# Split weights kept in an HBM scratch tensor, the mix's tanh ahead of the exponentials, and half of the hidden low parts on GpSimd

## The reference

```python
x = x + attn_a(layernorm(x))      # linear attention with a recurrence, 32 heads of 4
x = x + ffn(layernorm(x))         # 8 experts, summed
x = x + attn_b(layernorm(x))      # softmax attention, 16 query heads, one key head
x = x + ffn(layernorm(x))         # the same 8 experts again

def expert_step(acc, w):          # ffn; wg, wu: 128 x 512, wd: 512 x 128
    wg, wu, wd = w
    h = silu(x @ wg) * (x @ wu)
    return acc + h @ wd, None

mix = softmax((x @ Wmix.T + bmix).reshape(b, t, NH, 2), axis=-1)   # in attn_a
```

## Time and profile before

| | us |
|---|---|
| median of 3 runs | 1833.79 (1830.01 to 1835.16) |
| the profiled execution | 1834.89 |
| its span, first to last instruction | 1833.1 |
| mean granted clock of TensorE | 0.962 |
| DMA, mean over the span | 59 GB/s, 108.96 MB in all |

### The profile page before, as it was taken

The page is one execution under the profiler, slowest core; times in us unless marked ns, Lnnn a source line. Parts: engine busy times, 40 slices in busy tenths (PEclk is TensorE's granted clock), DMA queues, the critical chain, the costliest instruction groups (busy, mean ns, idle before and its releaser), DMA issues. The chain is left out here.

```text
span 1833.1 us, 25467 instructions
## 1 busy us (share of the span) xinstructions
PE 1653.8 (90%) x7232; PEld 1256.6 (69%) x7232; DVE 1188.0 (65%) x1999; ACT 1195.3 (65%) x2231; POOL 1235.1 (67%) x1025
## 2 busy tenths in 40 slices
PE   3597989888998989998699999996999999999998
PEld 2365766667676767786366666664788888888887
DVE  5668788786959677564466666662555555555554
ACT  2245565756575655776287787785677777777776
POOL 3576676767776667767177777776566666666665
PEclk8799999999999999999699999998999999999999
DMA  3011222212122222332000000000233333333331
GB/s 116 1 52 53 69 58 64 69 52 70 58 64 66 67 58 69 105 93 63 1 1 1 1 2 0 1 1 18 71 100 96 102 94 100 103 92 103 94 98 52
DMA packets 115177, 108.96 MB, mean 59 GB/s; under 512 B 7003, under 2 KB 81888, under 8 KB 115040
## 3 DMA queue, kind: packets, MB, share of 16 engines
q1 hardware_dynamic: 115040, 107.39, 19.8%
HBM read 105.27 MB, written 2.10 MB: 59 GB/s over the span
## 5 line engine op out<-in xcount | busy, mean ns | idle before, releaser
L465 POOL TENSOR_TENSOR ARENA_R<-ARENA,ARENA_R 128x512 fp32r<-128x512 f32 x384 | 558.7, 1457 | 347.3 <-ACT ARENA_R L460 345.5
L557 DVE TENSOR_TENSOR ARENA<-ARENA,pair 128x512 f32<-128x512 f32 x512 | 349.2, 682 | 407.6 <-PE pair L340 341.0
L517 ACT ACTIVATE ARENA<-bank 128x512 f32<-128x512 f32 x512 | 304.9, 595 | 305.8 <-PE bank L340 305.0
L338 PE MATMUL pair<-ARENA_R 128*128 128x512 f32 x1064 | 423.8, 398 | 54.0 <-ACT ARENA L919 24.4
L340 PE MATMUL pair<-ARENA_R 128*128 128x512 f32 x1064 | 417.0, 392 | 0.0
L339 PE MATMUL pair<-ARENA_R 128*128 128x512 f32 x1064 | 417.0, 392 | 0.0
L527 ACT ACTIVATE ARENA_R<-ARENA 128x512 fp32r<-128x512 f32 x512 | 319.5, 624 | 89.4 <-DVE ARENA L557 88.5
L533 DVE TENSOR_TENSOR ARENA_R<-ARENA,ARENA_R 128x512 fp32r<-128x512 f32 x384 | 314.7, 820 | 0.0
L842 POOL TENSOR_TENSOR ARENA_R<-ARENA,ARENA_R 128x512 fp32r<-128x512 f32 x192 | 249.4, 1312 | 80.3 <-ACT ARENA L1027 76.8
L338 PEld LDWEIGHTS pair<-ARENA_R 128*128 128x128 f32 x1064 | 201.9, 190 | 118.7 <-ACT ARENA L919 27.7
L338 PE MATMUL bank<-ARENA_R 128*128 128x512 f32 x568 | 241.1, 424 | 21.6 <-DVE ARENA L1503 15.6
(11 more groups left out here) (213 smaller groups left out, 2201.1 us busy)
## 6 DMA issues: line engine op xcount, KB each, us to landing
ARENA<-in_L_ffn_Wg_dram SPq DMA_DIRECT2D x128, 256.0 KB, 2.6
ARENA<-in_L_ffn_Wu_dram SPq DMA_DIRECT2D x128, 256.0 KB, 2.6
ARENA<-in_L_ffn_Wd_dram SPq DMA_DIRECT2D x128, 256.0 KB, 2.7
X<-in_L_attn_a_x_dram SPq DMA_DIRECT2D x8, 256.0 KB, 5.4
out_dram<-X SPq DMA_DIRECT2D x8, 256.0 KB, 3.4
CST<-in_tables_dram SPq DMA_DIRECT2D x1, 835.5 KB, 4.6
ARENA<-in_tables_dram SPq DMA_DIRECT2D x1, 768.0 KB, 4.6
CST<-in_tables_dram SPq DMA_DIRECT2D x1, 256.0 KB, 4.7
```

The costliest lines, as they stand in the source:

```text
L338: pe.matmul(dst, wh, xh, start=start, stop=False)
L465: g.tensor_tensor(WL[:, x % 2, part, :], WS[:, x % 2, part, :], WH[:, x % 2, part, :].bitcast(F32), ALU.subtract).then_inc(F.wl, 1)
L517: act.activation(SG[:, c % 2, :], bank[c % 2], ACT.Silu).then_inc(F.sil, 1)
L557: v.tensor_tensor(HF[:, c % FC, :], SG[:, c % 2, :], bank[2 + c % 2], ALU.mult).then_inc(F.mul, 1)
```

## The change

A scratch tensor `split_weights` in HBM holds for each of the eight experts and three parts the high and the low part side by side (512 KB a part). WH and WL become one buffer W2 of the same total size, two experts deep. Only for x < 8, the first feed-forward tile, are weights split on the chip; SyncE then stores each part (`store_split`). After all stores have landed, SyncE loads the split parts of expert x % 8 straight into W2 (`load_split`), each when TensorE has finished that part of expert x - 2. TensorE waits for the load instead of for GpSimd (`weights_ready`). The splitting at the end of attention b goes; the first load of block two waits there for the last `stack2` (q2_ready), as the splitting did.

`hidden_lo` is made by VectorE for even steps and by GpSimd for odd ones. The mix's tanh moves from step 10 to step 8, ahead of the exponentials. The projection v3 moves from step 11 to step 12.

```diff
--- before.py
+++ after.py
@@ -275,8 +275,7 @@
 
         XTH = take(2, TOK, dt=F32R)
         XTL = take(2, TOK, dt=F32R)
-        WH = take(2, 3, FFN, dt=F32R)
-        WL = take(2, 3, FFN, dt=F32R)
+        W2 = take(2, 3, 2, FFN, dt=F32R)
         HH = take(FC, TOK, dt=F32R)
         HL = take(FC, TOK, dt=F32R)
         LAH = take(12, P, dt=F32R)
@@ -313,7 +312,7 @@
         b_used = {n: sem(f"b_{n}_used") for n in BPROJ}
         B = sems("b", "u_q u_k hi lo v_ready v_used st_ready st_used kst_ready kst_used row_ready row_used nmh nml "
                       "q2_ready q2_used t_ready t_used pl vhi pv os turn oc ro o ot otc out done")
-        F = sems("f", "wload0 wload1 wh wl gate up sil mul hh hl hlp d ys back done")
+        F = sems("f", "wload0 wload1 store0 store1 sg su sd wh wl gate up sil mul hh hl hlp d ys back done")
         stored = sem("stored")
         carried = sem("carried")
 
@@ -322,6 +321,7 @@
 
             eng.sem_inc(carried, 1)
 
+        split = nc.dram_tensor("split_weights", [NE, 3, P, 2, FFN], F32, kind="Internal").ap()
         x_tok = a_x.rearrange("b t c -> (b t) c").rearrange("(n s p) c -> p n s c", n=NT, p=P)
         o_tok = out.rearrange("b t c -> (b t) c").rearrange("(n s p) c -> p n s c", n=NT, p=P)
 
@@ -439,7 +439,7 @@
 
         def lo_done(G):
 
-            return (F.hlp, G // FC + 1) if G % FC == FC - 1 else (F.hl, (FC - 1) * (G // FC) + G % FC + 1)
+            return (F.hlp if G % 2 else F.hl, G // 2 + 1)
 
         def base(G):
             return 0 if G < NT * CH else NT * CH
@@ -457,19 +457,39 @@
 
             act.wait_ge((F.wload0, F.wload1)[x % 2], 48 * (x // 2 + 1))
             after(act, (F.gate, F.up, F.d)[part], FC * (x - 1))
-            act.activation(WH[:, x % 2, part, :], WS[:, x % 2, part, :], ACT.Copy).then_inc(F.wh, 1)
+            after(act, (F.store0, F.store1)[x % 2], 48 * (x // 2))
+            act.activation(W2[:, x % 2, part, 0, :], WS[:, x % 2, part, :], ACT.Copy).then_inc(F.wh, 1)
 
         def lo_part(g, x, part):
 
             g.wait_ge(F.wh, 3 * x + part + 1)
-            g.tensor_tensor(WL[:, x % 2, part, :], WS[:, x % 2, part, :], WH[:, x % 2, part, :].bitcast(F32),
-                            ALU.subtract).then_inc(F.wl, 1)
+            g.tensor_tensor(W2[:, x % 2, part, 1, :], WS[:, x % 2, part, :],
+                            W2[:, x % 2, part, 0, :].bitcast(F32), ALU.subtract).then_inc(F.wl, 1)
+
+        def store_split(sp, x, part):
+
+            sp.wait_ge(F.wl, 3 * x + part + 1)
+            sp.dma_start(split[x, part], W2[:, x % 2, part, :, :].bitcast(F32)).then_inc((F.store0, F.store1)[x % 2], 16)
+
+        def load_split(sp, x, part):
+
+            landed = (F.sg, F.su, F.sd)[part]
+            after(sp, landed, 16 * (x - NE))
+            sp.wait_ge((F.gate, F.up, F.d)[part], FC * (x - 1))
+            sp.dma_start(W2[:, x % 2, part, :, :].bitcast(F32), split[x % NE, part]).then_inc(landed, 16)
+
+        def weights_ready(pe, x, part):
+
+            if x < NE:
+                pe.wait_ge(F.wl, 3 * x + part + 1)
+            else:
+                pe.wait_ge((F.sg, F.su, F.sd)[part], 16 * (x - NE + 1))
 
         def part_at(f, c):
 
             x = NE * f + c // FC + 1
             part = c % FC - 1
-            return None if part < 0 or x == NE * NT or x == 2 * NE * NT else (x, part)
+            return None if part < 0 or x >= NE else (x, part)
 
         def ffn_pe(pe, f, c):
 
@@ -478,14 +498,14 @@
             if c == 0:
                 pe.wait_ge(n_f.lo, f + 1)
             if k == 0:
-                pe.wait_ge(F.wl, 3 * x + 1)
+                weights_ready(pe, x, 0)
             after(pe, F.sil, G - 1)
-            split_product(pe, bank[c % 2], WH[:, u, 0, cols], WL[:, u, 0, cols], XTH[:, f % 2, :],
+            split_product(pe, bank[c % 2], W2[:, u, 0, 0, cols], W2[:, u, 0, 1, cols], XTH[:, f % 2, :],
                           XTL[:, f % 2, :]).then_inc(F.gate, 1)
             if k == 0:
-                pe.wait_ge(F.wl, 3 * x + 2)
+                weights_ready(pe, x, 1)
             after(pe, F.mul, G - 1)
-            split_product(pe, bank[2 + c % 2], WH[:, u, 1, cols], WL[:, u, 1, cols], XTH[:, f % 2, :],
+            split_product(pe, bank[2 + c % 2], W2[:, u, 1, 0, cols], W2[:, u, 1, 1, cols], XTH[:, f % 2, :],
                           XTL[:, f % 2, :]).then_inc(F.up, 1)
             if G - 3 >= base(G):
                 down(pe, G - 3)
@@ -497,9 +517,9 @@
             if c == 0:
                 after(pe, F.ys, G // CH)
             if k == 0:
-                pe.wait_ge(F.wl, 3 * x + 3)
+                weights_ready(pe, x, 2)
             pe.wait_ge(*lo_done(G))
-            split_product(pe, bank[4], WH[:, u, 2, cols], WL[:, u, 2, cols], HH[:, k, :], HL[:, k, :],
+            split_product(pe, bank[4], W2[:, u, 2, 0, cols], W2[:, u, 2, 1, cols], HH[:, k, :], HL[:, k, :],
                           start=(c == 0), stop=(c == CH - 1)).then_inc(F.d, 1)
 
         def back(pe, f):
@@ -542,7 +562,7 @@
         def ffn_pool(g, f, c):
 
             G = CH * f + c
-            if c % FC == 0 and G - 1 >= base(G):
+            if c % 2 == 0 and G - 1 >= base(G):
                 hidden_lo(g, G - 1)
             if part_at(f, c):
                 lo_part(g, *part_at(f, c))
@@ -555,7 +575,7 @@
             if G >= FC:
                 v.wait_ge(*lo_done(G - FC))
             v.tensor_tensor(HF[:, c % FC, :], SG[:, c % 2, :], bank[2 + c % 2], ALU.mult).then_inc(F.mul, 1)
-            if G - 1 >= base(G) and (G - 1) % FC != FC - 1:
+            if G - 1 >= base(G) and (G - 1) % 2 == 0:
                 hidden_lo(v, G - 1)
 
         def residual(v, f):
@@ -656,7 +676,14 @@
                         load_part(sp, n - 2, part)
             sp.dma_start(CST[:, CB:], consts[:, CB:CS]).then_inc(ld.tables_b, 16)
             sp.dma_start(WOB[:, :], b_Wo).then_inc(ld.bb, 16)
-            for x in range(2, 2 * NE * NT):
+            for x in range(NE):
+                for part in range(3):
+                    if x + 2 < NE:
+                        load_part(sp, x + 2, part)
+                    store_split(sp, x, part)
+            sp.wait_ge(F.store0, 24 * NE)
+            sp.wait_ge(F.store1, 24 * NE)
+            for x in range(NE, 2 * NE * NT):
                 if x == NE * (NT - 2) + 6:
                     sp.wait_ge(A.z, NT)
                     sp.wait_ge(A.done, NT)
@@ -669,8 +696,10 @@
                     sp.wait_ge(pr.ones, 4)
                     sp.dma_start(BB[0:2, 0:C], row(b_bo).broadcast_to([2, C])).then_inc(ld.bb, 16)
                     sp.dma_start(BB[0:2, C:], row(b_bv).broadcast_to([2, DB])).then_inc(ld.bb, 16)
+                if x == NE * NT:
+                    sp.wait_ge(B.q2_ready, 2 * NSEQ)
                 for part in range(3):
-                    load_part(sp, x, part)
+                    load_split(sp, x, part)
                 if x >= NE * (NT + 1) and x % NE == 6:
                     n = x // NE - NT - 1
                     sp.wait_ge(F.done, NT + n + 1)
@@ -845,9 +874,6 @@
                         b_rstd(g, t + 2)
                     if closing(t, b, k, (0, 3)):
                         one_rstd(g, n_f, NT, MV3, SM3)
-                    for part in range(3):
-                        if closing(t, b, k, (0, 8 + part)):
-                            lo_part(g, NE * NT, part)
                     if nxt.real() and (b, k) in ((0, 9), (1, 1)):
                         i, name = (0, "q") if b == 0 else (1, "k")
                         after(g, b_used[name], nxt.n + 1)
@@ -908,16 +934,15 @@
                     if c == 4:
                         half_tanh(t, 1)
                     if c == 8:
+                        act.wait_ge(a_ready["mx"], t + 1)
+                        after(act, A.wgt, t)
+                        act.activation(MIX[:, :], bank[5][:, 0:SEQ], ACT.Tanh, bias=BMIXD[:, 1:2],
+                                       scale=0.5).then_inc(a_used["mx"], 1)
                         elu_exp(t, 0)
                         elu_exp(t, 1)
                     if c == 9:
                         elu_relu(t, 0)
                         elu_relu(t, 1)
-                    if c == 10:
-                        act.wait_ge(a_ready["mx"], t + 1)
-                        after(act, A.wgt, t)
-                        act.activation(MIX[:, :], bank[5][:, 0:SEQ], ACT.Tanh, bias=BMIXD[:, 1:2],
-                                       scale=0.5).then_inc(a_used["mx"], 1)
                     if c == 27:
                         weight_rows(t, 0)
                     if c == 28:
@@ -1006,10 +1031,6 @@
                     if closing(t, b, k, (0, 7)):
                         act.wait_ge(B.v_ready, NT)
                         f_hi(act, NT, bank[0])
-                    for part in range(3):
-                        if closing(t, b, k, (0, 8 + part)):
-                            act.wait_ge(B.q2_ready, 2 * NSEQ)
-                            hi_part(act, NE * NT, part)
```

(2 more changed lines are left out.)

## The result

| | before | after |
|---|---|---|
| median of 4 runs, us | 1834.47 (1830.01 to 1837.0) | 1751.85 (1751.14 to 1753.8) |
| span of the profiled execution | 1833.1 | 1749.9 |
| granted clock of TensorE, mean | 0.962 | 0.969 |

A forecast was written before the change was run, and what follows sets the result against it. TensorE, busy 90%, bounds the kernel; time is won where it stands still, mainly in mixed tiles. Terms 42 + 3 - 1 + 4 + 8 - 1.3 + 3.8 = 58.5 us from 1834.9 give 1776 us, range 1754 to 1806.

The forecast's parts named there:

- the clock at 2.6 us: Mixed tiles (feed-forward of t-2 under attention of t): TensorE's clock dips follow stalls, in three of five tiles; 2.6 us won.
- The cut from 43.5 to 42: Mixed tiles: their summed gain lowered from 43.5 to 42 us, as a stall removed lets TensorE run into the next.
- The tanh, 14.4: Mixed tiles, step 10: TensorE's stop behind the mix's tanh goes, 2.89 us a tile, 14.4 for five.
- v3, 7 of 9.1: Mixed tiles: v3 one step later mostly covers TensorE's wait for key_value; of 9.1 us, 2 stay.
- Splitting: L557 11, GpSimd's product 4, weight_rows 3, others 1.5: Mixed tiles: us won from TensorE's waits behind VectorE's product (L557), GpSimd's product, weight_rows and others, without weight splitting.
- The bounds: Mixed tiles: 18 us won from only the tanh and half of key_value; 62 from every wait, its restart and all dips.
- Rival (a): Every stall goes: 20 us more won in the mixed tiles, 1756 us; chance 0.10.
- The low part at no cost: hidden_lo on GpSimd takes 1.28 us against 0.69 on VectorE; the extra 0.6 us are hidden by over 4 us.
- Rival (b): GpSimd's moved hidden_lo may hold VectorE's scans: mixed tiles win only 18 us, t = 2 loses 3; 1806 us, chance 0.13.
- t = 2, t = 8, block two, attention b: Outside the five mixed tiles: 3 - 1 us, 4 us, 8 us, and -1.3 + 3.8 us won.
- Loads at no cost: Split-weight loads of 512 KB: at most 64% of queues, 5.2 us to landing at worst, hidden with 4 us over.
- rival (c): Weights come late: parts landing later than 9.5 us stop TensorE once per expert; 1974 us at 12 us; chance 0.04.

The follow-up runs named there:

- no_low: The changed kernel with three of four hidden_lo on VectorE, as before the change: 1751.65 us, ratio 0.955 to the kernel before.
- skip runs: The changed kernel with 21 dummy GpSimd subtractions or memsets per mixed tile, none in steps 5 to 7: 1795.73 us and 1761.42 us.

## Why the prediction was right and where it failed

**Sign and mechanism** stood: TensorE's stops in the mixed tiles, 25 of the 54 us behind VectorE, which GpSimd held. **The step that failed is the last of the mixed tiles' terms, the clock at 2.6 us**: it was the only term for what stops do to TensorE's busy time, apart from the tanh's, and that time fell by 18.3 us. The cut from 43.5 to 42 went the wrong way too.

- *The tanh, 14.4.* Right: no wait behind it is left. Its place is worth 16.6 in the changed kernel and 12 in the one before.
- *v3, 7 of 9.1.* Too much: 2.7 were won and 6.4 stayed. A covered step doesn't help when the product that v3 waits for is itself late in VectorE's queue.
- *Splitting: L557 11, GpSimd's product 4, weight_rows 3, others 1.5.* Measured 13.3, 8.6, 2.6 and 2.5. (The working let seven of ten low parts stay on VectorE and four leave; six stay.) A third of the holding was taken to go and half of the product's wait to stay; the relief in VectorE's stretch from the product of step 10 to that of step 25 was 10.5 us (52.5 to 42.0) where 7.9 was worked out.
- All waits together: 40.9 forecast, 43.4 measured. That is 2.5 of the 20 us missing; 15.7 are the next term, and 1.5 are the cut to 42.
- *The clock, 2.6.* Measured 18.3, TensorE's busy time beyond what the matmuls need. In the tiles at clock 1.00 it fell from 89.1 to 86.7, 12 us over five, as stops went; the three tiles with dips (t = 3, 5 and 7, five dips in all) held 6 more. The forecast took the full price of a stop, 2.89 against the listed 2.73, for the tanh alone, and the listed wait for the other 36 stops. The list has 26 stops fewer after (41 to 15), 7 us at 0.27. In t = 4 two gaps of under 0.15 us, too short for the list, held another 0.5 us, which would be near 3 over five tiles; where the last 2 us come from was not traced. With 0.27 for each stop that it took to go and 6 for the dips, its sum would have been near 54, an estimate.
- *The bounds.* "Every wait, its restart and all dips" was put at 62. Just 62.0 were won, with 10.6 us of waits still there, so this bound was too low, for the same reason.
- *Rival (a), every stop goes, 1756, with 0.10*: its time came nearest, by luck. Its mechanism is not what ran: 15 stops are left, 9.1 of their 10.6 us behind VectorE, as the argument against it had said (VectorE's work at 2.4 us a step against TensorE's 2.2). The 20 us came from TensorE's busy time.
- *The low part at no cost*: right in the changed kernel, where no_low and the change are equal. Rival (b)'s mechanism is there (2.7 us more a tile for scans and phi), but pays less than the low parts that leave VectorE. With the splitting left in place the move costs 21 us, and there by another way, TensorE's waits for GpSimd's late work. GpSimd was busy for 83% of t = 4 then, and for 53% in the change; nothing between was tried.
- *What was not seen*: VectorE's wait in step 9 for GpSimd's addition to X. It was in the trace of before, 1.16 us at 346.23. It carried no term, though step 9 alone fell from 3.7 to 2.4 us in the mixed tiles, and both skip runs bind that to GpSimd's queue.
- *t = 2, t = 8, block two, attention b*: 1.8 for 2, 5.0 for 4, 10.3 for 8, 4.1 for 2.5. In block two the stop went wholly (TensorE busy 66.30 of 66.30), 1.2 us a tile.
- *"Every engine at full clock"* in block two: the rows give a granted clock for TensorE alone, 1.00.
- *Loads at no cost*: right, rival (c) fell. In 1300 to 1367 they land in 5.0 us at 55.4% of the queues, where 3 to 5 and 50 to 60% had been said; no wait of TensorE stands behind one in the change.

## What to carry to other kernels

A list of waits is not the price of the stops: add to each what the distance between starts around it shows, and the stretches at half clock behind some of the long ones. Work taken from a side engine can pay in three ways (its reads no longer hold the neighbour, its queue no longer makes others late, the stops of the bound engine go with their tails). Runs with dummy work in its place show that each is there; to size them apart, the dummies must differ in one thing alone, and these differed in length as well. A change of order helps more when the engine next in the chain has room; here the same two lines were worth 12 us before that room was made and 16.6 after.

## What the runs showed of the hardware

- The granted clock fell to 0.50 after a stop of 2.75 us (0.8 us behind its end) and stayed for 3.4 us (448.80 to 452.20 of the kernel before), with 0.43 us between matmuls of 512 columns instead of 0.23. After the same stop in t = 4 (2.73 us) it stayed at 1.00.
- 24 reading instructions of GpSimd, 37.1 us long, made VectorE's scans, low parts and phi in t = 4 5.3 us longer, 0.22 us for each (0.27 over the five tiles). So one of them doesn't block VectorE for its whole 1.55 us in the mean, as rival (b) had it for the worst case.
- The holding goes both ways: beside the subtractions GpSimd's own products of S took 1.70 us and its low parts 1.55, beside the memsets 1.29 and 1.43.
- A GpSimd copy of 128x512 took 0.91 us against 1.55 for a subtraction in the same place, and a memset of three times the size 1.38. VectorE's low parts were nearly as long beside the short copies as beside the subtractions (998 and 1021 ns over the five tiles). Why was not tried.
